# Gate parameters loaded behind the adjacency and prepared in layer 1, and TensorE's filler products spread over the first quarter, in a four-layer graph network kernel

## What is computed

```python
rank = jnp.cumsum(mask, axis=1); k = jnp.minimum(deg, 100.0)
w = mask * jnp.where(rank - (deg - k) > 0, 0.5 ** (deg - rank), 0.0)
x = _layernorm(x + w @ (x @ weight) + bias)
def _ggc(x, adj, W, wih, whh, bih, bhh):       # twice, with relu
    m = adj @ (x @ W)
    gi, gh = m @ wih.T + bih, x @ whh.T + bhh
    r, z = sigmoid(i_r + h_r), sigmoid(i_z + h_z)
    n = tanh(i_n + r * h_n)
    return (1 - z) * n + z * x
x = _layernorm(x + relu(_ggc(relu(_ggc(x, ...1)), ...2)))
x = _layernorm(x + (D^-.5 (adj + I) D^-.5) @ x @ W)
x = _layernorm(x + concat([x, adj @ x / (deg + 1)]) @ W.T)
```

## Time and profile before

| | us |
|---|---|
| median of 3 runs | 440.96 (440.83 to 441.45) |
| the profiled execution, device time | 440.98 |
| its span in the trace | 439.2 |
| TensorE matmuls busy | 414.7 (94%) |
| VectorE busy | 306.9 (70%) |
| ScalarE busy | 202.4 (46%) |
| GpSimd busy | 114.4 (26%) |

### The profile page before, as it was taken

The page is one execution under the profiler, slowest core; times in us unless marked ns, Lnnn a source line. Parts: engine busy times, 40 slices in busy tenths (PEclk is TensorE's granted clock), DMA queues, the critical chain, the costliest instruction groups (busy, mean ns, idle before and its releaser), DMA issues.

```text
span 439.2 us, 6391 instructions
## 1 busy us (share of the span) xinstructions
PE 414.7 (94%) x2254; PEld 198.3 (45%) x2254; DVE 306.9 (70%) x898; ACT 202.4 (46%) x325; POOL 114.4 (26%) x154
## 2 busy tenths in 40 slices
PE   6778998998999999999999999999999999999991
PEld 1222442344344434455555555555545454445481
DVE  3398779867977997466764647687848757477873
ACT  2447777876687777516543533443312222112100
POOL 9212214111420010024212202433424343401111
PEclk9889999999999999999999999999999999999997
DMA  8999999999999997000102010000000010100000
GB/s 111 107 158 108 107 107 108 107 168 113 111 112 112 108 107 81 1 12 13 24 14 25 13 25 0 3 0 1 1 0 13 16 21 15 36 13 24 16 27 21
DMA packets 25039, 23.71 MB, mean 54 GB/s; under 512 B 14512, under 2 KB 16432, under 8 KB 25008
## 3 DMA queue, kind: packets, MB, share of 16 engines
q0 software_dynamic: 9360, 16.78, 38.1%
q1 hardware_dynamic: 15360, 6.33, 6.6%
q10 hardware_dynamic: 288, 0.20, 0.2%
HBM read 69.44 MB, written 1.05 MB: 160 GB/s over the span
## 4 chain that ended last, share of the span: by engine, by line
PE 64%; DMA 25%; DVE 3%; POOL 3%; issue 2%; ACT 0%; POOLq 0%
PE Y L1004 44%; DMA adjT<-in_adjT 25%; PE both L902 7%; PE Y L881 3%; PE both L860 2%; PE both L863 2%; PE Y L893 2%; POOL rstd L264 1%; POOL adjT L292 1%; PE both L909 1%; PE both L855 1%; PE both L867 1%; PE Y L1010 0%; DVE stat L478 0%; DVE work L482 0%
## 5 line engine op out<-in xcount | busy, mean ns | idle before, releaser
L1004 PE MATMUL Y<-adjT,S 128*128 128x512 fp8e4 (+1 forms) x1056 | 231.7, 373 | 0.1
L1004 PEld LDWEIGHTS Y<-adjT,S 128*128 128x128 f16 x1056 | 101.7, 98 | 109.4 <-POOL S L279 1.2
L377 ACT ACTIVATE wgt<-both,consts 128x512 int16<-128x512 f32 x128 | 85.1, 687 | 33.3 <-PE both L902 29.9
L264 POOL TENSOR_TENSOR rstd<-stat,mhalf 128x4 f32<-128x4 f32 (+2 forms) x29 | 36.1, 1246 | 159.7 <-DVE stat L484 159.7
L902 PE MATMUL both<-adjT,fix 128*128 128x512 fp8e4 x160 | 62.5, 390 | 7.2 <-DMA adjT<-in_adjT 6.4
L902 PE MATMUL both<-adjT,tri 128*128 128x512 fp8e4 x160 | 62.7, 392 | 0.0
L881 PE MATMUL Y<-wgt,S 128*128 128x512 bf16 x160 | 62.0, 388 | 0.0
L505 DVE SCALAR_TENSOR_TENSOR work<-Y,yT 64x512 f32<-64x512 f32 x30 | 20.8, 694 | 50.9 <-ACT yT L336 50.5
L292 POOL DMA_DIRECT2D adjT<-in_adjT x63 | 34.4, 576 | 79.7 <-DMA adjT<-in_adjT 79.7
L336 ACT ACTIVATE yT<-Y 64x512 f32<-64x512 f32 x30 | 17.6, 587 | 78.6 <-PE Y L1004 53.9
L902 PEld LDWEIGHTS both<-adjT,fix 128*128 128x128 bf16 x160 | 15.8, 99 | 50.4 <-ACT wgt L377 28.6
(11 more groups left out here) (122 smaller groups left out, 443.8 us busy)
## 6 DMA issues: line engine op xcount, KB each, us to landing
adjT<-in_adjT POOLq DMA_DIRECT2D x63, 256.0 KB, 40.2
out_rows<-xrow SPq DMA_DIRECT2D x7, 128.0 KB, 1.9
xrow<-in_xrow SPq DMA_DIRECT2D x1, 640.0 KB, 8.0
x<-in_w_gates SPq DMA_DIRECT2D x1, 512.0 KB, 11.6
biases<-in_biases SPq DMA_DIRECT2D x1, 384.0 KB, 7.4
x<-S SPq DMA_TRANSPOSE x24, 2.4
xrow<-in_xrow SPq DMA_DIRECT2D x1, 256.0 KB, 4.2
adjT<-in_adjT POOLq DMA_DIRECT2D x2, 128.0 KB, 6.0
```

What stands on the lines that cost most here:

```text
L264: nc.gpsimd.tensor_tensor(rstd[:, 0:blocks], stat[:, 2, 0:blocks], mhalf[:, 0:blocks], ALU.pow)\
L377: nc.scalar.activation(wgt[:, c, tiles % 2, :], V[c][:, :], ACT.Relu, **({"bias": tile_bias[sums]} if sums else {})).then_inc(w_ready[c], 1)
L1004: mm = nc.tensor.matmul(bank(layer, g)[:, 0:nb * P], S[layer % 2][:, jb, :], cols[:, jb, :], start=(jb == 0), stop=(jb == JB - 1), skip_gr ...
```

## The change

The diff, cut to what matters; `BETWEEN` is shown by a line of it, since the rows below tell it better:

```diff
@@ SyncE
-            sp.wait_ge(load[NLOAD - 1], 32)
+            sp.wait_ge(load[14], 64)
             sp.dma_start(biases[:, D:13 * D], ...).then_inc(biases_in, 16)
             sp.dma_start(gate_pack, a["w_gates"]).then_inc(gate_in, 16)
             for layer in TURNS:
                 for g in range(G):
                     sp.wait_ge(s_ready, layer * G + g + 1)
+                    if layer == 1 and g == G // 2:
+                        sp.wait_ge(gate_const, 4)
@@ VectorE
-                if q == 2:
-                    gate_weights()
...
             rows0(Q - 1)
             split_rows0(Q - 1)
+            gate_weights()
@@ TensorE
-            for _ in range(6):
+            for _ in range(10):
                 nc.tensor.matmul(V[0][:, :], cutw[:, :], ones[:, :], start=True, stop=True)
...
-                {(7, 0): ((6, 3, 0), (6, 3, 1), (6, 2, 0), (6, 2, 1)), (7, 1): ((6, 1, 0), (6, 1, 1)), ...
+                {(2, 0): ((11,),), (5, 0): ((3,),), (5, 1): ((6, 3, 0), (6, 3, 1)), (6, 1): ((6, 2, 0), (6, 2, 1)), ...
...
-                    if q == 3:
-                        pe.wait_ge(gate_const, 4)
-                if q == 2 and s == 20 and c == 0:
-                    (the two products of w_m and w_i)
...
+                    elif len(entry) == 1:
+                        for _ in range(entry[0]):
+                            nc.tensor.matmul(Y[2][:, :], cutw[:, :], ones[:, :], start=True, stop=True)
...
-                        if q == 0 and s == STEPS.index(("quad", MASKED[0])):
-                            for _ in range(8):
-                                nc.tensor.matmul(Y[2][:, :], cutw[:, :], ones[:, :], start=True, stop=True)
...
+            def gate_sums():
+                pe.wait_ge(gate_in, 16)
+                for l in range(2):
+                    mm = nc.tensor.matmul(gates[0][:, 2 + l, 0:3 * D], w_m[0:D, l, :], w_i[0:D, l, :], start=True, stop=True)
+                    mm.then_inc(gate_prod, 1)
             def open_gates():
                 pe.wait_ge(rows0_ready, Q)
+                pe.wait_ge(gate_const, 4)
...
             def layer1():
-                product(1, 2, 0, 1)
                 combine(0, 6)
-                product(1, 2, 1, 2)
                 combine(0, 7)
-                product(1, 2, 2, 24)
-                product(1, 3, 0, 10)
-                open_gates()
+                gate_sums()
+                product(1, 2, 0, 24)
+                product(1, 3, 0, 7)
                 product(1, 0, 24, 32)
-                product(1, 1, 24, 32)
+                product(1, 1, 24, 31)
+                open_gates()
+                product(1, 1, 31, 32)
                 product(1, 2, 24, 32)
-                product(1, 3, 10, 11)
+                product(1, 3, 7, 22)
                 combine(1, 0)
```

More of the change, by code:

```diff
@@ L525, in rows0 @@
                 dve.wait_ge(combined, 2 * q + 2)
-                both_halves(lambda h: nc.vector.tensor_tensor(wide[0][:, h * B:(h + 1) * B, :], rowsum(0, h),
+                both_halves(lambda h: nc.vector.tensor_tensor(wide[0][:, h * B:(h + 1) * B, :], gates[0][:, h, :].rearrange("p (b d) -> p b d", d=D),
                                                               pair[:, h * B:(h + 1) * B, :], ALU.add))
@@ L684, in gate_weights @@
                 dve.wait_ge(gate_prod, 2)
-                prod = gates[0][:, 0:4:2, 0:3 * D]
+                prod = gates[0][:, 2:4, 0:3 * D]
                 did(nc.vector.tensor_scalar(wm16[:, :, 0, :], prod, GATE, None, ALU.mult))
@@ L854, in combine @@
                     if layer == 0:
-                        mm = nc.tensor.matmul(rowsum(0, g % 2)[:, b, :], y, w_y[:, 3 * D:4 * D], start=True, stop=True)
+                        mm = nc.tensor.matmul(gates[0][:, g % 2, b * D:(b + 1) * D], y, w_y[:, 3 * D:4 * D], start=True, stop=True)
                     if layer in (1, 2):
@@ L1027, in layer1 @@
             def layer1():
-                product(1, 2, 0, 1)
                 combine(0, 6)
-                product(1, 2, 1, 2)
                 combine(0, 7)
-                product(1, 2, 2, 24)
-                product(1, 3, 0, 10)
+                gate_sums()
+                product(1, 2, 0, 24)
+                product(1, 3, 0, 7)
+                product(1, 0, 24, 32)
+                product(1, 1, 24, 31)
                 open_gates()
-                product(1, 0, 24, 32)
-                product(1, 1, 24, 32)
+                product(1, 1, 31, 32)
                 product(1, 2, 24, 32)
-                product(1, 3, 10, 11)
+                product(1, 3, 7, 22)
                 combine(1, 0)
-                product(1, 3, 11, 25)
+                product(1, 3, 22, 32)
+                product(1, 4, 0, 4)
                 combine(1, 1)
-                product(1, 3, 25, 32)
-                product(1, 4, 0, 7)
+                product(1, 4, 4, 18)
                 combine(1, 2)
-                product(1, 4, 7, 21)
+                product(1, 4, 18, 32)
                 combine(1, 3)
-                product(1, 4, 21, 32)
-                product(1, 5, 0, 17)
+                product(1, 5, 0, 14)
                 combine(1, 4)
-                product(1, 5, 17, 32)
+                product(1, 5, 14, 32)
                 product(1, 6, 0, 17)
```

## The result

The changed kernel takes 438.58 us (median of 4 runs, 438.51 to 439.08), the kernel before 440.89 us in the same comparison (4 runs, 440.46 to 441.45): ratio 0.9949, 95% interval 0.9932 to 0.9967. That is 2.3 us, or 0.5%, faster; 438.9 was forecast. The profiled execution took 438.52 us with a span of 436.7.

The account below looks back on a forecast made before the run. Adjacency arrival up to pair 42 at about 118.7 us, then TensorE's work, was taken as the bound. Two ended waits give -2.08 us, all other terms 0: 440.98 - 2.08 = 438.9 us, own range 438.4 to 440.0.

Parts of the forecast that it names:

- What bounds the kernel: Adjacency arrival until pair 42 at about 118.7 us, then TensorE's work; ending waits of 1.37 and 0.71 us gives -2.08 us.
- The two loads therefore cost the stream 2.54 us: Gate loads behind pair 31: pairs 32 to 36 take 14.90 us instead of 12.36; moved, pairs 32 to 62 land 2.54 earlier.
- I credit none of that to the change: Slower stream after pair 36 (2.66, then 2.60 us a pair), cause unknown; no gain from it counted.
- Pair 58: Step 10 of quarter 3, next possible late pair: TensorE there at 157.55 us, wait 0 to 0.5 us, taken as 0.
- The gate weights in time: Gate loads issued behind pair 62 (166 to 169 us), in SBUF by 180.5, wanted at 184.5: 4.0 us to spare.
- The seam: Between the layers: three new or nearer waits met with 0.1, 0.55 and 0.54 us clearance; cost 0, range 0 to 0.6 us.
- The first quarter: New fillers and masked product places, all ahead of the wait before 75.61 us, where TensorE is 1.24 us early: 0.
- clock 1.00 from about 15 us: Sign in the profile after: TensorE's granted clock, 0.83 to 0.94 of full from 10 to 40 us before, held up by fillers.
- The rival that the clock counts: First quarter bounds the kernel, so full clock gains 3.4 us more: 435.5 us; chance 0.05 with anything else below 438.4.
- That pairs 32 to 36 are slow by themselves: Rival: the gate loads cost the stream nothing, so time stays 441.0 us; chance 0.12 together with all gain eaten.
- That the waits come back: Rival: small clearances are missed, in part or whole, 439.9 to 441.8 us; chance 0.10 for 440.0 to 440.9.
- the preparation bounds layer 1: Rival: VectorE's six gate operations end late and hold `open_gates`; 442.4 us if 4 us late; slower has chance 0.07.

Follow-up runs that it names:

- e5: Changed kernel with the two gate loads issued behind pair 31 again, but all layer 1 transposes behind pair 62: 439.33 us, ratio 0.9960 to the kernel before.
- e9: Changed kernel with the transposes of groups 0 to 3 of layer 1 issued ahead of the gate loads, which stay behind pair 62: 439.51 us, ratio 0.9964.
- e3: Kernel before with one edit, the two gate loads waiting for pair 42 instead of pair 31; gate preparation stays in quarter 2: 439.42 us, ratio 0.9965.
- e4: Changed kernel with `open_gates` back at its old place, ahead of the last eight row tiles of groups 0 to 2: 441.04 us, ratio 1.0.
- e2: Changed kernel with the old first quarter: 6 and 8 fillers and the masked products at their old places: 438.95 us, ratio 0.9950.
- e8: The changed kernel itself run again, unedited, as reference for later runs: 438.80 us, ratio 0.9948 to the kernel before.
- e6: Changed kernel without any filler products, masked products at their new places: 439.33 us, ratio 0.9958 to the kernel before.
- e1: Changed kernel with the two gate loads behind pair 31 again, the first transposes moving with them in SyncE's queue: 441.06 us, ratio 1.0.
- e7: Kernel before with 256 KB more loaded behind pair 31, half the gate array a second time: 441.94 us, ratio 1.0015.

## Why the prediction was right, and what it missed

**What bounds the kernel**: right. It is pair 26's landing plus TensorE's work, and the waits before pairs 38 and 42 were all that could be saved. They went, as forecast, for 2.08 us. The profiles differ by 2.3 us behind pair 26. The other 0.2 to 0.3 lie ahead of layer 1, since the first product behind the last `weigh` stands at 179.47 where 180.00 was worked out, and of this 0.53 us only 0.22 is the earlier landing of pair 26. Of the 0.31 left, 0.16 is the wait for pair 42, which was 0.87 us long and not the 0.71 of its bracket; the rest are small gaps of TensorE in quarters 2 and 3. That those are gaps for ScalarE's weights was argued and not shown.

**"The two loads therefore cost the stream 2.54 us"**: about right as a size (2.2 in e5), but "I credit none of that to the change" was wrong for what came behind. The slow pace of pairs 37 to 47 comes from the transposes, and the change moves these too, because they stand behind the loads in SyncE's queue. The step that I left out is that of the queue: I followed the two loads past pair 62, but not what is queued behind them. It did no harm to the sum, since the loads' leaving alone would have ended both waits (e9), as the working said. But it would have been close: where 0.46 us of clearance at pair 42 was worked out, e9 has about 0.1, as GpSimd's issue at 117.17 comes 0.12 us behind TensorE's step at 117.05, and before the change it came 0.24 behind the step that waited. With the transposes gone too it is more than 1.3 us (issue at 114.94, step at 116.32).

**Pair 58**: the forecast of 0 held, with more room than I gave it, though TensorE comes to its step at 157.02 where 157.55 was worked out. Pair 47 landed at 127.3, where 132.01 - 2.54 = 129.5 was worked out, because of the transposes again. e3 shows that this place was rightly named: there it takes 0.60 us.

**The gate weights in time**: right, by 14 us instead of 4: the load took 6.3 us instead of 11.6, and it was issued at 164.24, 4.3 us before the 168.5 worked out for pair 62 and outside the 166 to 169 named as a sign. The pace of 2.60 us a pair that the working used was that of a stream with transposes in it.

**The seam**: right in all three clearances: 0.2 (0.1 forecast), 0.65 (0.55) and 0.7 us (0.54). `combine(1, 0)` stands at 200.9 (201.3 forecast). e4 shows what the second is worth. `combine(1, 4)` starts at 218.29 us instead of 221.38, 3.1 us earlier where 2.7 was forecast.

**The first quarter**: 0 was right (e2). The forecast of "clock 1.00 from about 15 us" held in one execution and not in the other: 20 to 40 us had 0.94 and 0.89 in this profile and 1.00 in that of e8, with 361.3 us behind pair 26 in both. And the wait for pair 26 was to grow; it shrank from 1.24 to 0.22 us (0.50 in e8), since TensorE was ready for that pair at 75.17 us instead of 74.37. Half of this is the last pair it waits for before that, at 38.87 instead of 38.48 us. The other half comes from the new places of the masked products: from there to the same step of quarter 1, all at clock 1.00, TensorE takes 26.69 us (also in e8), and 26.27 in the kernel before and 26.28 in e2 with the old places. In the changed kernel 0.35 us of it is a wait for ScalarE's `wgt` before 45.87 us, which those two don't have. So the new first quarter itself gives nothing and brings TensorE later to pair 26; it costs nothing because that pair comes later still.

**The rival that the clock counts** fell, in the form of 3.4 us gained: nothing was. Its mechanism is real on the other side, where no wait follows: e6's profile loses 0.64 us by it. It ran 1.68 us longer behind the gap at 38 us; the clearance to pair 26 and an earlier start took the rest. The Trainium skill's rule (TensorE: Matmul & The Clock Gate, Terms), the time at the lower rate times one minus the ratio, gives 1.7 us for it (0.3 + 1.4, by the clocks of 0.97 and 0.86). The trace agrees with it for that stretch, and not for the end of the kernel.

**The other rivals.** That pairs 32 to 36 are slow by themselves fell with the profile after and e1: the bulge is gone with the loads and back with them. That the waits come back, or the preparation bounds layer 1, fell by the clearances above. e3 and e4 show that both mechanisms are real in this kernel: 0.60 us for pair 58, 1.91 us at `open_gates`.

## What to carry to other kernels

A transfer that isn't needed yet costs what it takes from the stream only if some later piece of the stream is waited for; find that piece first, then move the transfer behind it, even if its consumer has to be moved for the last part. When an issue is moved in a queue that runs in order, everything behind it moves too and has a price of its own: here 1.5 us of stream beside the loads' 2.3. Filler work that holds the clock can pay only where no wait stands between it and the work that sets the end.

## What the runs showed of the hardware

Transposing transfers of 128 KB each (128 x 512 in fp16) beside a full stream took 18.1 us to land instead of 2.5 (medians; before, e5). Two of them, 256 KB, cost the stream 1.5 us (e9), where 256 KB of plain load cost 0.66 (e7) and the 896 KB of the gate loads 2.3 (e5). The Trainium skill (DMA: Bandwidth & Descriptors, Issuing engines are not separate DMA queues) says that transfers of all issuers interleave on the same engines. The trace agrees: GpSimd's pairs 32 to 36 took 14.56 instead of 12.36 us while SyncE's two loads ran (e5). That one sort holds the stream for more than twice as long as its bytes do as a plain load is what the rows add.
